# Feed-forward half: GELU layer over pairs of tiles, products from fp32r parts, output stored tile by tile

## The reference, cut to what matters

```python
def _layer(x, wqkv, qs, ksc, wo, lg, lb, w1, b1, w2, b2):
    h = shift_token(x)                 # second half of the channels from the token before
    q, k, v = jnp.split(h @ wqkv, 3, axis=-1)
    ...
    q = l2norm(q) * qs
    k = l2norm(k) * ksc
    q, k = rotary_xpos(q, k)
    o = local_attention(q, k, v)
    x = x + o @ wo
    h = shift_token(x)
    h = (h - mu) / jnp.sqrt(var + 1e-05) * lg + lb
    h = h @ w1 + b1
    a, g = jnp.split(h, 2, axis=-1)
    x = x + (a * jax.nn.gelu(g)) @ w2 + b2
```

## Time and profile before

| | |
|---|---|
| median of 3 runs | 3207.31 us (3207.3 to 3214.26) |
| the profiled execution | 3221.64 us, span 3219.8 us |
| mean granted TensorE clock | 0.964 of full |
| busy: TensorE | 3012.8 us (94%) |
| busy: VectorE, ScalarE, GpSimd | 2490.0 (77%), 2268.6 (70%), 780.4 us (24%) |
| feed-forward half | from about 1709 to 3201 us |

### The profile page before, as it was taken

The page is one execution under the profiler, slowest core; times in us unless marked ns, Lnnn a source line. Parts: engine busy times, 40 slices in busy tenths (PEclk is TensorE's granted clock), DMA queues, the critical chain, the costliest instruction groups (busy, mean ns, idle before and its releaser), DMA issues. The chain is left out here.

```text
span 3219.8 us, 63296 instructions
## 1 busy us (share of the span) xinstructions
PE 3012.8 (94%) x23672; PEld 1873.1 (58%) x23672; DVE 2490.0 (77%) x4820; ACT 2268.6 (70%) x4998; POOL 780.4 (24%) x1019
## 2 busy tenths in 40 slices
PE   8969999999999999999985999999999999999995
PEld 5733333333333333333354788888888888888884
DVE  4668899999989999899445767677777767777774
ACT  3407788888878888788875767676667767676663
POOL 4510000000000000000054434343434434343432
PEclk9958999999989999999997999999999999999998
DMA  3333212333322233322040000000000000000002
GB/s 115 112 82 41 38 25 41 41 41 41 41 32 32 40 41 41 41 41 41 12 161 23 1 1 0 0 0 0 0 1 35 1 1 0 0 0 0 0 1 71
DMA packets 47115, 99.37 MB, mean 31 GB/s; under 512 B 17184, under 2 KB 29472, under 8 KB 40480
## 3 DMA queue, kind: packets, MB, share of 16 engines
q1 hardware_dynamic: 42400, 95.48, 15.6%
q10 hardware_dynamic: 4544, 1.38, 0.2%
HBM read 71.13 MB, written 25.69 MB: 30 GB/s over the span
## 5 line engine op out<-in xcount | busy, mean ns | idle before, releaser
L691 DVE TENSOR_REDUCE mx<-aux 128x1 f32<-128x1024 f32 x1024 | 1246.5, 1224 | 116.4 <-PE aux L556 108.8
L661 ACT ACTIVATE probs<-scores 128x512 f32<-128x512 f32 x2048 | 1118.5, 597 | 250.1 <-PE scores L580 143.2
L556 PE MATMUL aux<-k_stack,q_stack 48*128 48x512 f32 x2048 | 792.8, 466 | 27.7 <-DMA k_stack<-qk_dram 19.5
L580 PE MATMUL scores<-q_stack,k_stack 50*128 50x512 f32 x2048 | 777.8, 456 | 13.4 <-ACT probs L661 13.4
L592 PE MATMUL pv<-probs,v_ones 128*32 128x256 f32 x8192 | 670.2, 400 | 0.1
L580 PEld LDWEIGHTS scores<-q_stack,k_stack 50*128 50x128 f32 x2048 | 317.3, 189 | 439.5 <-ACT probs L661 414.7
L592 PEld LDWEIGHTS pv<-probs,v_ones 128*32 128x32 f32 x8192 | 162.8, 109 | 373.6 <-ACT probs L661 275.8
L556 PEld LDWEIGHTS aux<-k_stack,q_stack 48*128 48x128 f32 x2048 | 320.5, 194 | 77.7 <-DVE mx L691 51.7
L522 POOL CAST m_parts<-head_max 128x16 fp32r<-128x16 f32 x32 | 6.3, 198 | 1355.9 <-DVE head_max L696 1355.9
L1241 PE MATMUL bank<-QO,w_sb 128*128 128x128 f32 x2816 | 328.2, 277 | 1.5 <-ACT QO L1328 1.5
L1241 PEld LDWEIGHTS bank<-QO,w_sb 128*128 128x128 f32 x2816 | 322.5, 193 | 2.5 <-ACT QO L1328 2.5
(11 more groups left out here) (175 smaller groups left out, 4628.2 us busy)
## 6 DMA issues: line engine op xcount, KB each, us to landing
q_stack<-qk_dram SPq DMA_DIRECT2D x192, 128.0 KB, 5.2
k_stack<-qk_dram SPq DMA_DIRECT2D x192, 128.0 KB, 6.8
qk_dram<-qkT_hi SPq DMA_DIRECT2D x32, 256.0 KB, 3.1
qk_dram<-qkT_lo SPq DMA_DIRECT2D x32, 256.0 KB, 3.6
out<-x_sb SPq DMA_DIRECT2D x9, 384.0 KB, 4.0
wqkv_sb<-in_wqkv SPq DMA_DIRECT2D x2, 1536.0 KB, 7.7
w_sb<-in_w SPq DMA_DIRECT2D x2, 1408.0 KB, 11.7
x_sb<-in_x SPq DMA_DIRECT2D x1, 2048.0 KB, 18.9
```

What stands on the lines that cost most here:

```text
L556: last = nc.tensor.matmul(aux[:, ring["unit"], block_of_keys % 2], q_stack[rows, r % BODY, tile * P:(tile + 1) * P], k_stack[rows, r % BOD ...
L580: nc.tensor.matmul(scores[:, item % BANKS1], k_stack[0:SCORE_ROWS, r % BODY, s * P:(s + 1) * P], q_stack[0:SCORE_ROWS, r % BODY, j * 512:( ...
L661: nc.scalar.activation(probs[:, item % PROBS], scores[:, item % BANKS1], ACT.Exp, scale=float(D1) ** -0.5).then_inc(probs_ready, 1)
L691: nc.vector.reduce_max(mx[:, slot, tile, half:half + 1], aux[:, unit].rearrange("p a k -> p (a k)"), AX.X).then_inc(max_taken, 1)
```

## The change

- **Weights**: all weights of the two layers come as one array in 30 pieces. During `attention_phase` each of the first 30 heads loads one piece of 576 columns, GpSimd splits it into rounded value and remainder, and SP stores both in `split_dram`. `Weights` keeps hi and lo of one layer; the second layer's are loaded over them in mid-run, each as its last reader frees it. The splits on ScalarE and VectorE at the start of the feed-forward half go.
- **Products**: F, H and Y are made from fp32r parts, three products for one. hT, H and F are made for two tiles together: hT on the pair's second tile (`SECOND_OF_PAIR`) with H0 to H2, H3 to H5 a step later (`FIRST`); F from the six in the following two steps. H0 to H5 hold the products a and gate of one chunk for 256 tokens each (H5 the rest).
- **Around them**: GpSimd makes `act_hi` and `act_lo` and so frees the H banks; ScalarE makes `hT` and `hT_hi`, VectorE `hT_lo` and `oT_lo`; ScalarE takes all four PT copies. VectorE normalises probabilities in two instructions for four, and makes `norm2` in two halves for one, k first; GpSimd makes `rnorm` in two halves.
- **Order**: TensorE's step is now scores, shift, k, q, F, PT0 to PT3, hT, v, oT, H, qT and kT, xT, Y. On VectorE the statistics of the last norm stand behind the cosine products and sums of k and q; on GpSimd they keep their place behind `x_b2`.
- **End**: `final_phase` goes. The last norm runs on tile t - 4 and t - 5; GpSimd adds x1 from a ring of two tiles that SP loads, and SP stores each tile. Two steps more are at the end.

```diff
+                if left > 1:
+                    sp.wait_ge(raw_split, r + 1)
+                    for part, tile in enumerate((raw_hi, raw_lo)):
+                        sp.dma_start(pieces_dram[n, part], tile[:].bitcast(F32)).then_inc(raw_stored, 16)
+                    sp.wait_ge(raw_stored, 32 * (r + 1))
...
+                if left > 1:
+                    pool.wait_ge(raw_loaded, 16 * (r + 1))
+                    nc.gpsimd.tensor_copy(raw_hi[:], raw[:]).then_inc(raw_rounded, 1)
+                    pool.wait_ge(raw_rounded, r + 1)
+                    nc.gpsimd.tensor_tensor(out=raw_lo[:], in0=raw[:], in1=raw_hi[:], op=ALU.subtract).then_inc(raw_split, 1)
...
+ITEMS = ([(f"S{j}", 1, "dve", 4 + j, None) for j in range(4)]
+         + [("shift", 0, "dve", 1, None), ("k", 2, "act", 2, None), ("q", 2, "act", 3, None), ("F", -3, "dve", 0, SECOND_OF_PAIR)]
+         + [(f"PT{j}", 1, "act", 4 + j, None) for j in range(4)]
+         + [("hT", 0, "act", 1, SECOND_OF_PAIR), ("v", 2, "act", 2, None), ("oT", 1, "act", 3, None)]
+         + [(f"H{j}", 0, "act", 4 + j, SECOND_OF_PAIR) for j in range(3)]
+         + [(f"H{3 + j}", -2, "act", 4 + j, FIRST) for j in range(3)]
+         + [("qT", 2, "act", 7, None), ("kT", 2, "act", 4, None), ("xT", 3, "act", 3, None), ("Y", 1, "dve", 1, None)])
...
+FREES = {"act": [(f"S{j}", 1, None) for j in range(4)] + [(f"PT{j}", 1, None) for j in range(4)] + [("v", 2, None), ("qT", 2, None), ("kT", 2, None)],
+         "dve": [("xT", 2, None), ("normed0", 1, None), ("normed1", 1, None), ("shift", 0, None), ("k", 2, None), ("q", 2, None),
+                 ("hT", 0, SECOND_OF_PAIR), ("F", -3, SECOND_OF_PAIR), ("oT", 1, None), ("Y", 1, None)],
+         "pool": [(f"H{j}", 0, SECOND_OF_PAIR) for j in range(3)] + [(f"H{3 + j}", -2, FIRST) for j in range(3)]}
...
+            for i in range(3):
+                sp.wait_ge(wqkv_free[i], 1)
+                weights.load_wqkv(sp, split_dram, i, 1)
+            sp.wait_ge(wo_free, 1)
+            weights.load_wo(sp, split_dram, 1)
+            sp.wait_ge(w1_free, 1)
+            weights.load_w1(sp, split_dram, 1)
+            sp.wait_ge(w2_free, 1)
+            weights.load_w2(sp, split_dram, 1)
...
+                if last_layer(-4)(st):
+                    n, slot = nth_last(st, -4), st.slot(-4, X1_SLOTS)
+                    if n >= X1_SLOTS:
+                        w.upto(x_summed, n - X1_SLOTS + 1)
+                    sp.dma_start(x1_ring[:, slot], x1_dram[:, st.tile(-4)]).then_inc(x1_loaded[slot], 16)
+                if last_layer(-5)(st):
+                    w.upto(x_summed, nth_last(st, -5) + 1)
+                    sp.dma_start(out_tiles[:, st.tile(-5)], x_sb[:, st.tile(-5)]).then_inc(out_stored, 16)
+            sp.wait_ge(out_stored, 16 * NT)
...
-                if last_layer(-2)(st):
-                    n = nth_last(st, -2)
+                if last_layer(-4)(st):
+                    n = nth_last(st, -4)
                     w.upto(fmv_made, n + 1)
-                    nc.gpsimd.tensor_scalar(fvar_eps[:], fmv[:, st.slot(-2), 1:2], EPS, None, ALU.add).then_inc(fvar_made, 1)
+                    nc.gpsimd.tensor_scalar(fvar_eps[:], fmv[:, st.slot(-4), 1:2], EPS, None, ALU.add).then_inc(fvar_made, 1)
                     w.upto(fvar_made, n + 1)
-                    nc.gpsimd.tensor_tensor(out=frstd[:, st.slot(-2)], in0=fvar_eps[:], in1=minus_half[:, 0:1], op=ALU.pow).then_inc(frstd_made, 1)
+                    nc.gpsimd.tensor_tensor(out=frstd[:, st.slot(-4)], in0=fvar_eps[:], in1=minus_half[:, 0:1], op=ALU.pow).then_inc(frstd_made, 1)
...
-                    w.upto(norm2_made, t + 3)
-                    nc.gpsimd.tensor_scalar(norm2_min[:], norm2[:], 1e-24, None, ALU.max).then_inc(norm2_floor, 1)
-                    w.upto(norm2_floor, t + 3)
-                    nc.gpsimd.tensor_tensor(out=rnorm[:, st.slot(2, 2)], in0=norm2_min[:], in1=minus_half[:], op=ALU.pow).then_inc(sin_rnorm_made, 1)
+                    for n, a in enumerate((1, 0)):
+                        w.upto(norm2_made, 2 * (t + 2) + n + 1)
+                        nc.gpsimd.tensor_scalar(norm2_min[:, a], norm2[:, a], 1e-24, None, ALU.max).then_inc(norm2_floor, 1)
+                        w.upto(norm2_floor, 2 * (t + 2) + n + 1)
+                        nc.gpsimd.tensor_tensor(out=rnorm[:, st.slot(2, 2), a], in0=norm2_min[:, a], in1=minus_half[:], op=ALU.pow).then_inc(sin_rnorm_made, 1)
+                if last_layer(-5)(st):
+                    n, x_tile = nth_last(st, -5), x_sb[:, st.tile(-5), :]
+                    w.upto(x_normed, n + 1)
+                    w.upto(x1_loaded[st.slot(-5, X1_SLOTS)], 16 * (n // X1_SLOTS + 1))
+                    nc.gpsimd.tensor_tensor(out=x_tile, in0=x_tile, in1=x1_ring[:, st.slot(-5, X1_SLOTS)], op=ALU.add).then_inc(x_summed, 1)
+                if st.exists(hidden_stage(st)):
+                    for j in range(3):
+                        piece, rows = pieces_of(st)[j]
+                        w.upto(hidden_made, 3 * (t - 1) + j + 1)
+                        nc.gpsimd.tensor_copy(act_hi[rows, piece], act_full[rows, j]).then_inc(hidden_rounded, 1)
+                        w.upto(hidden_rounded, 3 * (t - 1) + j + 1)
+                        nc.gpsimd.tensor_tensor(out=act_lo[rows, piece], in0=act_full[rows, j], in1=act_hi[rows, piece], op=ALU.subtract).then_inc(by_pool, 1)
...
+            def summands(pieces, begins):
+                out = bank("F")
+                for i in range(2):
+                    for p in pieces:
+                        rows = slice(0, P if p < HW else HR)
+                        for n, (a_part, w_part) in enumerate(((act_hi, w2_hi), (act_hi, w2_lo), (act_lo, w2_hi))):
+                            last = nc.tensor.matmul(out[:, i * C:(i + 1) * C], a_part[rows, p, i * P:(i + 1) * P], w_part[rows, p],
+                                                    start=(begins and i == 0 and p == pieces[0] and n == 0),
+                                                    stop=(not begins and i == 1 and p == pieces[-1] and n == 2), skip_group_check=True)
+                return last
...
+                if st.exists(hidden_stage(st)):
+                    d = hidden_stage(st)
+                    if st.tile_of_pair(0) == SECOND_OF_PAIR:
+                        read("hT", t)
+                        if starts_layer(st, -1) is not None:
+                            pe.wait_ge(w1_loaded, 32 * (starts_layer(st, -1) + 1))
+                    for piece, _ in pieces_of(st):
+                        out = begin(f"H{piece}", t + d)
+                        for i, chunk in enumerate((piece, HW + piece) if piece < HW else (2 * HW,)):
+                            for k in range(NC):
+                                for n, (w_part, h_part) in enumerate(((w1_hi, hT_hi), (w1_hi, hT_lo), (w1_lo, hT_hi))):
+                                    last = nc.tensor.matmul(out[:, i * PAIR:(i + 1) * PAIR], w_part[:, k, chunk * P:(chunk + 1) * P], h_part[:, k],
+                                                            start=(k == 0 and n == 0), stop=(k == NC - 1 and n == 2))
+                        end(last, f"H{piece}")
...
+                    out = begin("Y", t + 1)
+                    for c in range(4):
+                        for n, (o_part, w_part) in enumerate(((oT_hi, wo_hi), (oT_hi, wo_lo), (oT_lo, wo_hi))):
+                            last = nc.tensor.matmul(out[:, 0:C], o_part[:, c], w_part[:, c], start=(c == 0 and n == 0), stop=(c == 3 and n == 2))
+                    end(last, "Y")
...
+                if st.exists(hidden_stage(st)):
+                    d, layer = hidden_stage(st), st.layer(hidden_stage(st))
+                    for j, (piece, _) in enumerate(pieces_of(st)):
+                        src = item(f"H{piece}", t + d)
+                        if piece < HW:
+                            last = nc.scalar.activation(gate[:, j], src[:, PAIR:2 * PAIR], ACT.Gelu, bias=b1_sb[:, layer, HW + piece:HW + piece + 1])
+                        else:
+                            last = nc.scalar.activation(gate[0:HR, j], src[HR:P, 0:PAIR], ACT.Gelu, bias=b1_sb[HR:P, layer, 2 * HW:])
+                        last.then_inc(gate_made, 1)
...
+                    for n, (a, name) in enumerate(((1, "k"), (0, "q"))):
+                        w.upto(squares_made, 2 * (t + 2) + n + 1)
+                        nc.vector.tensor_tensor(qk_cos[:, a].rearrange("p (h d) -> p h d", d=D2), bank(name)[:].rearrange("p (h d) -> p h d", d=D2),
+                                                cos_table[:, st.table(2), a].unsqueeze(1).to_broadcast([P, H2, D2]), ALU.mult).then_inc(by_dve, 1)
+                        nc.vector.tensor_reduce(norm2[:, a], squares[:, a].rearrange("p (h d) -> p h d", d=D2), AX.X, ALU.add).then_inc(norm2_made, 1)
+                        if at == NT - 3:
+                            dve.drain().then_inc(wqkv_free[n], 1)
...
```

(33 more changed lines are left out.)

519 lines of the change are left out of this document (230 added, 289 removed).

## The result

The change makes the kernel slower, by 1.5%. The changed kernel takes 3255.43 us (median of 4 runs, 3247.74 to 3283.8), the kernel before 3210.78 us on the same chip (4 runs, 3207.3 to 3217.97): a ratio of 1.0152, 95% interval 1.0088 to 1.0217. I had forecast 3176 us and a range of 3112 to 3251. The profiled execution took 3252.39 us with a span of 3250.6, 30.8 us above the span of before.

What follows compares the result with a forecast made beforehand. The prediction took the feed-forward half to be bound by TensorE. Its terms, -91 + 73 - 6 - 10 + 3 = -31 us, taken from the median of 3207.31, gave 3176 us, range 3112 to 3251.

Steps and rivals of the forecast that it cites:

- start and attention: Feed-forward start: weight splits go, -6 us; attention: added weight split and transfers, +3 us.
- Tail: From t = 62 to the end, without the last stage: 57 us against 66.7, -10 us.
- First layer: Steps t = 0 to 36 of the feed-forward half: 716 us against 807, -91 us.
- Late steps: Steps t = 36 to 61, with the last norm moved in: 25.6 us each, 666 us against 593, +73 us.
- Part 1: F, H and Y from fp32r products 0.12 us apart: TensorE's work of a step from 21.5 to 19.6 us.
- Rival 5: Products of 256 columns take 0.22 us each, TensorE's step 25.9 us: 3385 us, chance 0.03.
- Part 2: Other engines keeping up in the first layer: waits and loop ends add 0.5 us, 20.1 us a step.
- Part 3: Late steps: GpSimd's work queues behind its fmv wait, delaying kT; 24.1 us a step, 25.6 with low clock, +73 us.
- rival 3: Late steps: TensorE at half clock from qT through the next scores, 28.3 us a step, 3246 us; chance 0.14.
- Rival 1: Late steps: the clock stays up in the gaps, 24.1 us a step, 3137 us; chance 0.20.
- Rival 2: Late steps: the wait for fmv is absorbed, 20.4 us a step, 3040 us; chance 0.07.
- Rival 4: SBUF port lock: GpSimd's powers hold off VectorE's rotation, 0.5 us a first-layer step, 1.2 a late one: 3225 us, chance 0.08.

Runs made afterwards that it cites:

- e11: e2 plus v and kT in other banks, x1's addition last, and VectorE's hidden-norm statistics one mask and maximum earlier: 3057.78 us, 0.947 of before.
- e1: Changed kernel with VectorE's fstats, fnmr and fmv moved right behind the step's mv, GpSimd's program untouched: 3111.71 us, 0.967 of before.
- e2: Changed kernel with GpSimd's fvar and frstd moved from in front of the x copy to behind the last subtraction: 3099.82 us, 0.9622 of before.
- e4: Changed kernel with transposes nobody reads filling TensorE's gaps in late steps, the wait for fmv kept: 3235.33 us, 1.0046 of before.
- e5: e2 with the probabilities normalised in four instructions over 512 elements instead of two over 1,024: 3094.68 us, 0.9597 of before.

## Why the prediction was wrong

**The sign.** -31 forecast, +31 measured between the two profiled spans. Term by term: start and attention -3 forecast, -2.2 measured, but out of larger parts. From TensorE's first instruction of the half to the scores of t = 0 it takes 34.1 us instead of 41.9, -7.8 where I took -6. TensorE's work in the attention takes 1444.1 us instead of 1436.0, at a granted clock of 0.96 and 0.95: +8.1 where I took +3. The other traces of the change have it longer still (1444.2 us and more), but there is one trace of before alone, so that term's size stays open, and the agreement of the sum is luck. Tail -10, measured -6.9. First layer -91, measured -74. Late steps +73, measured +114. The last two hold the miss: 17 and 41 us. Between 3176 us and the median of 3255.43 lie another 17 us that belong to no term: the profiled execution of before lay 14.3 above the median from which I counted, that of the change 3.0 below its own.

**Part 1 held.** F, H and Y products start 0.12 us apart, and TensorE's work is nearly what I counted: 20.70 and 19.0 us in e11, where it hardly waits, 19.85 on average against 19.6. Rival 5 is out.

**Part 2 was short.** A full turn of the loop takes 20.7 us a step, not 20.1: 0.25 is the work above. I had a wait of 0.4 us on a pair's first tile for kT, and 0.3 on the second for `hT_lo`. Measured, the first tile waits 1.1 us (20.13 against 19.0), mostly in front of v, whose bank is k's and free only behind VectorE's cos product: 11.1 us in 14 times. I had not followed v's bank at all. The second waits for nothing that counts, so both together make 0.55 a step against 0.35. And I took 0.15 us a step for loop ends; a step with one takes 21.95 instead of 20.70, so 0.3 over the four steps of a turn. That is 0.6 us a step, 22 over the layer, of which the short steps gave some 5 back.

**Part 3 had the right mechanism and was mis-sized.** The order in GpSimd's queue was the cause I named, and e1 and e2 show it. The step that failed is the time up to kT: I had a late step at 24.1 us with the clock up, and e4, where it is up, has 25.2. That is 29 of the 41 us.

In my sum `hn` was done at 8.7 us, `fmv` at 11.7 and kT free at 21.7; in the step shown they stand 9.9, 12.8 and 23.2 behind the scores, which start right behind Y, and in e4 9.4, 12.4 and 22.8 or 23.2. So `hn` is 0.7 us late before any low clock: VectorE waited 0.47 us for `rstd`, and the first half of `hn` took 0.75 us beside `x_b2` where it takes 0.42 in e5. I had no term for either. By the like pair `fvar` and `frstd` in the earlier trace rows (0.66 and 0.57) `rstd` would have been ready in time, but it took 1.61 and `var_eps` 1.30, as the change widens the normalisations that run beside them. The rest is behind `fmv`, 10.4 to 10.9 us to kT where I had 10.0, though GpSimd's own work was well priced (10.2; a power on 8 columns takes 1.93 and not 1.7). An earlier `rstd` in the changed kernel itself, with its order left as it is, was not tried.

The clock was the smaller miss. I took 1.5 us for it, as it "won't cover them in every step". It did cover them in every step, and reached into the scores: 4.0 us from kT to the scores instead of 2.25, and 0.46 in the scores. e4 prices it at 1.8, 0.3 us a step more or 8 of the 41 us. What is left, some 4 us, is about what the late steps with a loop end add (28.4 us each). No one of these misses turns the sign alone (-31 + 29 is still -2); the 29 of the chain and the 17 of the first layer together do.

**The rivals.** The time is that of rival 3, the other side: 27.2 us a step against its 28.3, above its break-even of 26.8, and 3246 us in all; I gave it 0.14. Its mechanism is half there. It put 4.2 us of low clock on a step of 24.1, and the runs show 1.8 on one of 25.2: qT's transposes still ran at full clock (0.66 us for four, kT's 1.11), and the step is long by its waits. So its figure is near in part by luck. Rival 1 is out by the windows (clock 0.91 and 0.89), and with the clock up the step is 25.2 us and not its 24.1. Rival 2 is out by GpSimd's 3.43 us of idle time in front of `fvar`; its step of 20.4 us came only when that order was changed (e2, 21.0).

**Rival 4, half right.** As I had it, the powers hold off the rotation, and they don't: the addition at 2129.86 took 0.69 us beside a power that ran from 2129.48 to 2131.47, and so did all 43 rotation additions that lay within a power between 1800 and 3000 us. But the reverse direction does hold: in the changed kernel `var_eps` took 1.30 us and `rstd` 1.61, each ending some 0.1 to 0.5 us behind a wide normalisation of 1.23, and e1, e5 and e11 show that whatever short instruction GpSimd has at that time is the long one, by as much as VectorE's instruction is wide. VectorE is held too where `x_b2` starts first: `hn`'s first half took 0.74 to 0.77 us in all 52 steps in which it stood beside `x_b2`, and the second wide product of e11 1.55 instead of 1.22. The Trainium skill (SBUF — State Buffer, sections "Terms" and "Who interferes with whom") says that a VectorE instruction with two SBUF inputs and a GpSimd one that reads SBUF take turns at a port pair, for the whole instruction, the first to start winning. With the normalisations the traces agree (1.30 us beside 1.23, 0.23 without one); with the rotation beside the power they don't (0.69, as alone). The measurement decides: the price was some 0.7 us up to the end of `hn`, not 1.2 behind it.

**Not tried.** The attention part without its weight split; with a start that moves by 30 us, a few runs could not settle a term of 3 or 8 us.

## What to carry to other kernels

A wait near the head of an in-order queue is priced by everything behind it. The value it waits for here is needed a whole step later, and moving two instructions to the end of GpSimd's program turned +1.5% into -3.8%. Price the short instructions at the head of such a chain by what runs beside them: the row from which `rstd` looked free was read beside a narrower product. When two gaps of 2 us appear in TensorE's every step, carry the low clock into every step (1.8 us here). A forecast near zero net gain turns on terms of this size: here no single one turned it, but two did. And follow every result into its bank: who frees it, and who stood in it before.
